# Moving the centring of V for the first two pairs from a TensorE matmul to VectorE and GpSimd

## The chip, the cores and the metric

The kernel runs on one core of one Trainium2 chip. The metric is the device time of one execution in microseconds (us). The engines are TensorE (PE in the profile), VectorE (DVE), ScalarE (ACT), GpSimd (POOL) and SyncE (SP), which here issues the DMAs.

## The reference

Eight sequences of 256 tokens with 512 features pass through one block. For each sequence: `x = x + mlstm(layernorm(x), ctx, ctx)` and then `x = x + ffn(layernorm(x))`.

- `mlstm` has 16 heads of 32 features. Gates come from `[q, k, v] @ Wi` and `@ Wf`; a cumulative sum of log-sigmoids and a running maximum give a decay matrix D; the scores `q k^T / sqrt(32)` are multiplied by D, divided by a normaliser, and multiplied with V. Each head's output of 32 features is then normalised (mean taken off, divided by the root of the variance) and multiplied by `ln_scale`.
- `ffn` has weights of 4 bits with a scale per group of 128: `silu(x Wg^T) * (x Wu^T)`, 1408 wide, then `Wd`, then division by the root mean square.

Because the mean over a head's 32 output features is taken off, the kernel takes the mean over each head's 32 features off V beforehand: the mean of the output is then zero.

## The kernel before, in words

The eight sequences are worked in four pairs (512 tokens, four tiles of 128 tokens). One call of `iteration(p, q, n)` on each engine has 22 half-steps `h`: in it the attention of pair `p` (eight units `u` of four heads each), the feed-forward of the pair before, `q`, and at its end the first part of the next pair, `n` (norm, transposes, gates, scans). The calls are (0, None, 1), (1, 0, 2), (2, 1, 3), (3, 2, None), (None, 3, None). Each engine has its own program in a fixed order written out by hand, and the engines meet at semaphores.

What the change touches:

- Pairs 2 and 3 centre V so: `v_means` on VectorE (L1275) sums each head's 32 features of `ctx_sb` and scales the sums by -1/32; `centre_v` on GpSimd (L514) adds them to `ctx_sb` and writes `v_sb`, in four instructions of 128x512.
- Pairs 0 and 1 centre V otherwise: a matrix `centre` is made by GpSimd at the start (`centring`, L490), TensorE multiplies the transposed context by it (`centre_v`, L907, 16 matmuls of 128x128 fp32), and ScalarE copies the four banks to `v_sb` (`read_v`, L664).
- `keep_busy(count)` on TensorE (L1168) is matmuls whose result is not used. They stand where TensorE would otherwise wait.
- `decode_up(i)` on VectorE (L1466, by `decode`, L1459) turns packed 4-bit weights to 16-bit values in three instructions. Four of eight come before `iteration(0, None, 1)`.
- `mask(p, u)` on GpSimd (L526) zeroes what lies above the diagonal of the decay matrix (L532, twice) and makes `vw` from `v_sb` (L543, twice). VectorE's `products` (L1322, L1329) wait for it, and so does TensorE's `state_sums` (L959).
- `scans(0)` on VectorE (L1296) make the running sums; its `nm_ready` (L1310) starts TensorE's `spread_first` (L1157) and SyncE's spreading of `negm`.
- `read_scales` (L776) and `fetch_exp` (L680) on ScalarE convert scales and fetch the table for Exp.

Of the kernel before, what the change touches and what calls it, by code (L numbers as in the profile page):

```python
# [32 lines left out]
P = 128  # L33
# [76 lines left out]
def xattn_ffn(nc, x, ctx, ctxT, w_gates, b_gates, ln_scale, gu_bytes, gu_scales, dn_bytes, dn_scales, out):  # L110
# [6 lines left out]
    with es:  # L117
# [28 lines left out]
        own_rows = sb("own_rows", [P, HG, DH + 1])  # L146
        centre = sb("centre", [P, P])
        later = sb("later", [P, 2, HG, DH + 1])
# [82 lines left out]

        def bank_v(p, tt):
            return pf[:, (0, 2)[tt]] if p == 0 and tt < 2 else pq[:, 1] if p == 0 and tt == 3 else \
                po[:] if tt == (3 if p else 2) else pf[:, tt]

        def bank_y(p, n):
# [38 lines left out]
        vmean_ready = sem("vmean_ready")  # L275
        centre_ready = sem("centre_ready")
        vc_done = sem("vc_done")
        v_ready = sem("v_ready")
# [191 lines left out]
        def _(pool):  # L470
# [18 lines left out]

            def centring():  # L490

                heads = centre[:].rearrange("q (h d) -> q h d", d=DH)
                pool.memset(centre[:], -1.0 / DH).then_inc(centre_ready, 1)
                pool.wait_ge(centre_ready, 1)
                pool.affine_select(out=heads, in_=heads, compare_op=ALU.is_ge, fill=0.0, base=0,
                                   pattern=[[-DH, HG], [0, DH]], channel_multiplier=1).then_inc(centre_ready, 1)
                pool.wait_ge(centre_ready, 2)
                pool.affine_select(out=heads, in_=heads, compare_op=ALU.is_ge, fill=0.0, base=DH - 1,
                                   pattern=[[DH, HG], [0, DH]], channel_multiplier=-1).then_inc(centre_ready, 1)
                pool.wait_ge(centre_ready, 3)  # L500
                pool.tensor_tensor(centre[:], centre[:], ident[:], ALU.add).then_inc(centre_ready, 1)

            def gate_weights():
# [9 lines left out]

            def centre_v(p):  # L514
                pool.wait_ge(am_ready, 2 * p + 2)
                take_wait(pool)
                pool.wait_ge(vmean_ready, p - 1)
                pool.wait_ge(s_ctx, 16 * p + 16)
                pool.wait_ge(pv_done, UNITS * p)
                for tt in range(TT):  # L520
                    m = vmean[:, 1, tt * NH:(tt + 1) * NH].unsqueeze(2).to_broadcast([P, NH, DH])
                    pool.tensor_tensor(v_sb[:, tt, :, 0:DH],
                                       ctx_sb[:, tt].rearrange("q (h d) -> q h d", d=DH), m, ALU.add
                                       ).then_inc(v_ready, 1)
# [68 lines left out]
            def iteration(p, q, n):  # L593
# [13 lines left out]
                if q is None:  # L607
                    by_ln_scale(p)
                    residual1(p)
                    norm2(p)  # L610
                    return
                gated(q, FT - 1)
# [19 lines left out]

            setup()
            centring()
            rstd1(0)
            gate_weights()
            mask(0, 0)
            iteration(0, None, 1)
            for p in range(1, PAIRS - 1):
# [6 lines left out]
        def _(act):  # L646
# [10 lines left out]
            def norm1(p):  # L657
# [4 lines left out]
                last.then_inc(xn_ready, 1)  # L662

            def read_v(p):  # L664

                if p == 1:
                    act.wait_ge(pv_done, UNITS)
                for tt in range(TT):
                    act.wait_ge(vc_done, TT * p + tt + 1)
                    act.activation(v_sb[:, tt, :, 0:DH], bank_v(p, tt).rearrange("q (h d) -> q h d", d=DH), ACT.Copy  # L670
                                   ).then_inc(v_ready, 1)

# [118 lines left out]
            def iteration(p, q, n):  # L791
# [37 lines left out]
                if n is not None:  # L829
                    read_xT(n)  # L830
                    if q is None:
                        read_v(n)
                if p is not None and q is not None:
# [17 lines left out]
            softplus(0)  # L851
            read_v(0)
            fetch_exp()
            read_scales()
            exps(0, 0, 0)
# [11 lines left out]
        def _(pe):  # L867
# [38 lines left out]

            def centre_v(p):  # L907

                pe.wait_ge(centre_ready, 4)
                if p == 1:  # L910
                    pe.wait_ge(o_read, UNITS)
                for tt in range(TT):
                    for k in range(KT):
                        last = pe.matmul(bank_v(p, tt)[:, k * P:(k + 1) * P], xT[:, KT + k, tt * P:(tt + 1) * P],
                                         centre[:], start=True, stop=True)
                    last.then_inc(vc_done, 1)

            def turn_back(p):
# [40 lines left out]
            def state_sums(p, q, u):  # L959

                hg, b = u // 2, u % 2
                pe.wait_ge(vw_ready, 2 * UNITS * p + 2 * u + 2)
                if u == 0 and p < 2:
                    pe.wait_ge(s_ctx, 16 * p + 16)
                if p == 0:
# [60 lines left out]
            def turn_y(p):  # L1026
                pe.wait_ge(yn_ready, p + 1)
                if p == 0:
                    pe.wait_ge(v_ready, 2 * TT)
                if p < PAIRS - 1:  # L1030
# [126 lines left out]
            def spread_first(half):  # L1157

                if half == 0:
                    pe.wait_ge(v_ready, TT)  # L1160
                    pe.wait_ge(nm_ready, 1)
                for hh in range(2):
                    r = 2 * half + hh
                    last = pe.matmul(pf[:, 2 * half + 1, hh * S:(hh + 1) * S],
                                     ident[0:ROWS, r:r + 1].to_broadcast([ROWS, P]), nm[:], start=True, stop=True)
                last.then_inc(bc_done, 1)
# [8 lines left out]
            def iteration(p, q, n):  # L1175
# [27 lines left out]
                if n is not None:  # L1203
                    if q is None:
                        keep_busy(21)
                    turn_x(n)
                    gate_sums(n)
                    if q is None:
                        centre_v(n)
                        keep_busy(16)  # L1210
                if q is not None:
# [13 lines left out]
            gate_sums(0)  # L1225
            centre_v(0)
            keep_busy(10)
            spread_first(0)
# [11 lines left out]
        def _(dve):  # L1240
# [34 lines left out]
            def v_means(p):  # L1275

                dve.wait_ge(s_ctx, 16 * p + 16)
                step(dve.tensor_reduce(vmean[:, 0], ctx_sb[:].rearrange("q t (h d) -> q (t h) d", d=DH),
                                      AX.X, ALU.add))
                dve.tensor_scalar(vmean[:, 1], vmean[:, 0], -1.0 / DH, None, ALU.mult).then_inc(vmean_ready, 1)  # L1280
# [213 lines left out]
            def iteration(p, q, n):  # L1494
# [29 lines left out]
                if q is None:  # L1524
# [7 lines left out]
                    low_yT(p)  # L1532
                    read_a(n)
                    return
                if q is not None:
# [35 lines left out]
            input_rows(0)  # L1571
            for i in range(UP_FIRST, UP_EARLY):
                decode_up(i)
            scans(0)
            read_a(0)
            norm1_sums(1)
            iteration(0, None, 1)
            dve.wait_ge(sc_ready, 2)

# [41 lines left out]
```

## Time and profile before

| | us |
|---|---|
| median of 3 runs | 519.88 (519.51 to 520.72) |
| the profiled execution | 519.88 |
| its span, first to last instruction | 518.2 |

| engine | busy us | share of the span |
|---|---|---|
| PE | 488.7 | 94% |
| DVE | 392.6 | 76% |
| POOL | 328.4 | 63% |
| ACT | 299.2 | 58% |

Busy time of a whole engine doesn't tell what a moved instruction costs; the timelines of the stretch around it do. In a timeline row the first number is the start, the second the time, then engine, line, operation, tile written <- tiles read, and shapes; `x4` means that four such instructions are merged; a bracket at the end tells how long the engine was idle before, and what ended that.

### The profile page before, as it was taken

The numbers are of one execution on the slowest core, as the hardware profiler recorded it, in microseconds if no ns is written. First come the engines' busy times: TensorE is split into PE (matmuls) and PEld (weight loads), VectorE is DVE, ScalarE is ACT, GpSimd is POOL, SyncE is SP. The second block draws the span as 40 slices with busy tenths as digits, with TensorE's granted clock in tenths as the row PEclk, the third lists the DMA queues.
The fourth block names the chain that finished last, engine by engine and source line by source line (L and its number), as shares of the span: only waits on it lengthen the run. The fifth ranks groups of instructions, "written<-read, shape, count | busy, mean of one in ns | idle before, by whom it ended". The sixth has DMA issues, their size and how long they took to land.

```text
span 518.2 us, 8362 instructions
## 1 busy us (share of the span) xinstructions
PE 488.7 (94%) x2821; PEld 290.4 (56%) x2821; DVE 392.6 (76%) x690; ACT 299.2 (58%) x648; POOL 328.4 (63%) x368
## 2 busy tenths in 40 slices
PE   8899989589999899999999999999999989999996
PEld 3668766347666344567775445477774444444442
DVE  5968999779888988378888899378888952999411
ACT  1558764588776252588877245588875123877210
POOL 3025565088886764578887883778877771999610
PEclk9979999899999999999999999999999999999999
DMA  8685064372103300267006000663000000200011
GB/s 273 197 253 193 1 217 171 112 279 64 38 1 116 128 2 1 84 244 245 2 3 243 1 0 4 216 239 116 2 0 3 20 20 20 102 0 2 1 41 40
DMA packets 18507, 47.81 MB, mean 92 GB/s; under 512 B 1696, under 2 KB 4640, under 8 KB 17440
## 3 DMA queue, kind: packets, MB, share of 16 engines
q1 hardware_dynamic: 18464, 47.28, 26.4%
q8 instruction: 22, 0.36, 0.3%
q14 instruction: 21, 0.17, 0.1%
HBM read 37.31 MB, written 4.33 MB: 80 GB/s over the span
## 4 chain that ended last, share of the span: by engine, by line
PE 66%; DVE 20%; ACT 5%; issue 4%; POOL 3%; DMA 1%; SPq 0%; DVEq 0%; POOLq 0%; ACTq 0%
PE pf L1152 19%; PE pf L1088 12%; PE pf L1126 7%; PE pq L955 5%; PE po L1017 3%; PE pq L1111 3%; PE pf L1111 3%; DVE ffn L1430 3%; ACT dmat L715 3%; DVE ffn L1434 2%; DVE dmat L1329 2%; PE pq L1022 1%; DVE th L1442 1%; PE pq L903 1%; DVE w_down L1491 1%
## 5 line engine op out<-in xcount | busy, mean ns | idle before, releaser
L573 POOL TENSOR_TENSOR ffn<-ffn,ts 128x512 f32<-128x512 f32 x88 | 119.6, 1365 | 40.1 <-DVE ffn L1434 37.2
L1088 PE MATMUL pf<-yT,gu_val 128*128 128x512 f16 x464 | 135.9, 381 | 2.9 <-ACT ts L749 1.1
L1152 PE MATMUL pf<-w_down,hT 128*128 128x512 f32 x264 | 115.9, 595 | 1.7 <-DVE w_down L1491 1.7
L749 ACT ACTIVATE ts<-pf,gu_scale 128x512 f32<-128x512 f32 x134 | 85.1, 684 | 9.6 <-PE pf L1088 4.8
L1152 PEld LDWEIGHTS pf<-w_down,hT 128*128 128x128 f32 x264 | 49.3, 190 | 62.6 <-issue 57.5
L715 ACT ACTIVATE dmat<-negm,aT 128x128 f32<-128x128 f32 x248 | 77.6, 392 | 1.9 <-DMA negm<-negm_dram 1.9
L1088 PEld LDWEIGHTS pf<-yT,gu_val 128*128 128x128 f16 x464 | 56.0, 127 | 35.1 <-DVE ffn L1434 3.9
L532 POOL TENSOR_SCALAR_AFFINE_SELECT dmat<-dmat 128x512 f32<-128x512 f32 x64 | 43.4, 692 | 43.8 <-ACT dmat L715 43.8
L578 POOL TENSOR_TENSOR hT<-ffn,th 128x512 f32<-128x512 f32 x44 | 57.8, 1317 | 15.2 <-DVE th L1442 15.2
L1017 PEld LDWEIGHTS po<-v_sb,dmat 128*128 128x128 f32 x384 | 63.1, 191 | 4.6
L1017 PE MATMUL po<-v_sb,dmat 128*128 128x33 f32 x384 | 58.3, 233 | 0.0
L1434 DVE SCALAR_TENSOR_TENSOR ffn<-pf,gu_scale,ffn 128x512 f32<-128x512 f32 x67 | 50.3, 751 | 7.2
L1430 DVE SCALAR_TENSOR_TENSOR ffn<-pf,gu_scale,ts 128x512 f32<-128x512 f32 x67 | 49.7, 742 | 3.5 <-ACT ts L749 3.1
L767 ACT ACTIVATE th<-pf 128x512 f32<-128x512 f32 x16 | 9.5, 592 | 68.2 <-PE pf L1152 40.6
L955 PE MATMUL pq<-xT 32*128 32x128 f32 x448 | 40.9, 301 | 1.8
L1442 DVE SCALAR_TENSOR_TENSOR th<-th,ffn 128x512 f32<-128x512 f32 x44 | 41.3, 944 | 0.1
L584 POOL TENSOR_SCALAR ms<-ssq 128x1 f32<-128x1 f32 x16 | 4.4, 275 | 57.2 <-ACT th L767 56.9
L1329 DVE SCALAR_TENSOR_TENSOR dmat<-pq,dmat 128x512 f32<-128x512 f32 x56 | 35.9, 682 | 4.4 <-PE pq L955 3.3
L1126 PE MATMUL pf<-w_down,hT 128*128 128x512 f32 x88 | 39.1, 592 | 0.0
L955 PEld LDWEIGHTS pq<-xT 32*128 32x128 f32 x448 | 30.1, 189 | 12.1 <-PE pq L955 7.0
L722 ACT ACTIVATE tok<-po 128x264 f32<-128x264 f32 x32 | 12.5, 391 | 35.2 <-PE pq L1022 25.4
L758 ACT ACTIVATE th<-ffn 128x512 f32<-128x512 f32 x44 | 27.5, 626 | 5.8 <-POOL ffn L573 5.8
(156 smaller groups left out, 795.4 us busy)
## 6 DMA issues: line engine op xcount, KB each, us to landing
negm<-negm_dram SPq DMA_DIRECT2D x31, 512.0 KB, 5.1
xT<-in_ctx_T SPq DMA_DIRECT2D x4, 1024.0 KB, 7.9
ctx_sb<-in_ctx SPq DMA_DIRECT2D x4, 1024.0 KB, 5.4
x_sb<-in_x SPq DMA_DIRECT2D x4, 1024.0 KB, 5.9
x_res<-x_sb SPq DMA_DIRECT2D x4, 1024.0 KB, 4.6
out<-x_res SPq DMA_DIRECT2D x16, 256.0 KB, 2.0
ffn<-in_x SPq DMA_DIRECT2D x3, 1024.0 KB, 9.2
ts<-in_gate_up_bytes SPq DMA_DIRECT2D x4, 352.0 KB, 9.4
```

The source lines that it names most:

```text
L573: pool.tensor_tensor(acc, acc, ts[:, h % TDEEP, 1], ALU.add).then_inc(tsum_ready, 1)
L578: pool.tensor_tensor(hT[:, j], acc_buf(q, 1, j), th[:, j % 2], ALU.mult).then_inc(h_ready, 1)
L715: last = act.activation(dmat[:, u % 2, half, c, hh], m[:, c * P:(c + 1) * P], ACT.Exp, bias=aT[:, c, bh:bh + 1])
L749: act.activation(ts[:, h % TDEEP, g], bank(q, h, g), ACT.Copy, scale=gu_scale[:, g * GU + o:g * GU + o + 1]).then_inc(t_ready, 1)
L955: last = pe.matmul(bank_qk(p, u, half)[:, c:c + P], xT[r, KT + hg, t0:t0 + P], xT[r, hg, t0:t0 + P], start=True, stop=True)
L1017: pe.matmul(po[:, col:col + DH + 1], dmat[:, u % 2, half, blk, hh], v_sb[:, 2 * b + blk, hg * HG + 2 * half + hh], start=True, stop=True)
L1088: ins = pe.matmul(bank(q, h, g), gu_val[:, h // 2 + h % 2 * FT, g], yT[:, part, g], start=(part == 0), stop=(part == 1))
L1126: last = pe.matmul(pf[:, tt], hT[:, j, tt * P:(tt + 1) * P], w_down[:, j], start=(j == 0), stop=(j == FT - 1))
L1152: last = pe.matmul(pf[:, tt], hT[:, j, tt * P:(tt + 1) * P], w_down[:, j], start=(j == 0), stop=(j == FT - 1))
L1430: dve.scalar_tensor_tensor(acc, bank(q, h, 2), gu_scale[:, 2 * GU + o:2 * GU + o + 1], ts[:, h % TDEEP, 0], ALU.mult, ALU.add).then_inc(ac ...
L1434: dve.scalar_tensor_tensor(acc, bank(q, h, 3), gu_scale[:, 3 * GU + o:3 * GU + o + 1], acc, ALU.mult, ALU.add).then_inc(acc_ready, 1)
L1442: dve.scalar_tensor_tensor(th[:, j % 2], th[:, j % 2], 1.0, acc_buf(q, 0, j), ALU.add, ALU.mult).then_inc(gg_ready, 1)
```

## The change

For pairs 0 and 1 it does what pairs 2 and 3 do already. `centre`, `centring`, TensorE's `centre_v` and ScalarE's `read_v` go. GpSimd's `centre_v(0)` stands in two halves around `mask(0, 0)`, and `centre_v(1)` at the end of `iteration(0, None, 1)`. `v_means(0)` stands between `input_rows(0)` and `scans(0)`, where `decode_up(3)` was; `decode_up(3)` moves behind `norm1_sums(1)`. `v_means(1)` stands behind `read_a(1)`. The counts of `keep_busy` go from 10 to 28 and from 16 to 36. ScalarE reads the scales before it fetches the table. TensorE's waits on the context's DMA and on `v_ready` before `spread_first` and `turn_y` go.

```diff
@@ -144,7 +144,6 @@
         vw = sb("vw", [P, 2, HG, DH + 1])
         state = sb("state", [P, 2, HG, DH + 1])
         own_rows = sb("own_rows", [P, HG, DH + 1])
-        centre = sb("centre", [P, P])
         later = sb("later", [P, 2, HG, DH + 1])
         decay = sb("decay", [P, 2, NH])
         yT = sb("yT", [P, 2, KT, TT * P], F16)
@@ -229,10 +228,6 @@
         def bank_state(p):
             return pf[:, 1] if p == 0 else pq[:, 1]
 
-        def bank_v(p, tt):
-            return pf[:, (0, 2)[tt]] if p == 0 and tt < 2 else pq[:, 1] if p == 0 and tt == 3 else \
-                po[:] if tt == (3 if p else 2) else pf[:, tt]
-
         def bank_y(p, n):
             return po[:] if n == 2 else pq[:, min(n, 2)]
 
@@ -273,8 +268,6 @@
         nb_ready = sem("nb_ready")
         xn_ready = sem("xn_ready")
         vmean_ready = sem("vmean_ready")
-        centre_ready = sem("centre_ready")
-        vc_done = sem("vc_done")
         v_ready = sem("v_ready")
         xT_done = sem("xT_done")
         xT_read = sem("xT_read")
@@ -487,19 +480,6 @@
                                    ).then_inc(const_ready, 1)
                 pool.wait_ge(const_ready, 7)
 
-            def centring():
-
-                heads = centre[:].rearrange("q (h d) -> q h d", d=DH)
-                pool.memset(centre[:], -1.0 / DH).then_inc(centre_ready, 1)
-                pool.wait_ge(centre_ready, 1)
-                pool.affine_select(out=heads, in_=heads, compare_op=ALU.is_ge, fill=0.0, base=0,
-                                   pattern=[[-DH, HG], [0, DH]], channel_multiplier=1).then_inc(centre_ready, 1)
-                pool.wait_ge(centre_ready, 2)
-                pool.affine_select(out=heads, in_=heads, compare_op=ALU.is_ge, fill=0.0, base=DH - 1,
-                                   pattern=[[DH, HG], [0, DH]], channel_multiplier=-1).then_inc(centre_ready, 1)
-                pool.wait_ge(centre_ready, 3)
-                pool.tensor_tensor(centre[:], centre[:], ident[:], ALU.add).then_inc(centre_ready, 1)
-
             def gate_weights():
 
                 pool.wait_ge(s_const, 16 * 2)
@@ -511,13 +491,14 @@
                 pool.wait_ge(var1_ready, p + 1)
                 pool.tensor_tensor(rs[:, 0], vv[:, 0], neghalf[:, 0:TT], ALU.pow).then_inc(rstd1_ready, 1)
 
-            def centre_v(p):
+            def centre_v(p, tiles=range(TT)):
                 pool.wait_ge(am_ready, 2 * p + 2)
                 take_wait(pool)
-                pool.wait_ge(vmean_ready, p - 1)
+                pool.wait_ge(vmean_ready, p + 1)
                 pool.wait_ge(s_ctx, 16 * p + 16)
-                pool.wait_ge(pv_done, UNITS * p)
-                for tt in range(TT):
+                if not (isinstance(p, int) and p == 0):
+                    pool.wait_ge(pv_done, UNITS * p)
+                for tt in tiles:
                     m = vmean[:, 1, tt * NH:(tt + 1) * NH].unsqueeze(2).to_broadcast([P, NH, DH])
                     pool.tensor_tensor(v_sb[:, tt, :, 0:DH],
                                        ctx_sb[:, tt].rearrange("q (h d) -> q h d", d=DH), m, ALU.add
@@ -608,6 +589,7 @@
                     by_ln_scale(p)
                     residual1(p)
                     norm2(p)
+                    centre_v(n)
                     return
                 gated(q, FT - 1)
                 if n is not None:
@@ -631,10 +613,11 @@
                 down_scale(q, 3)
 
             setup()
-            centring()
             rstd1(0)
             gate_weights()
+            centre_v(0, range(2))
             mask(0, 0)
+            centre_v(0, range(2, TT))
             iteration(0, None, 1)
             for p in range(1, PAIRS - 1):
                 iteration(p, p - 1, p + 1)
@@ -660,15 +643,6 @@
                     last = act.activation(xg[:, tt], xg[:, tt], ACT.Identity, bias=nb[:, tt:tt + 1],
                                           scale=rs[:, 0, tt:tt + 1])
                 last.then_inc(xn_ready, 1)
-
-            def read_v(p):
-
-                if p == 1:
-                    act.wait_ge(pv_done, UNITS)
-                for tt in range(TT):
-                    act.wait_ge(vc_done, TT * p + tt + 1)
-                    act.activation(v_sb[:, tt, :, 0:DH], bank_v(p, tt).rearrange("q (h d) -> q h d", d=DH), ACT.Copy
-                                   ).then_inc(v_ready, 1)
 
             def softplus(p):
 
@@ -828,8 +802,6 @@
                     down_squares(q, 1)
                 if n is not None:
                     read_xT(n)
-                    if q is None:
-                        read_v(n)
                 if p is not None and q is not None:
                     down_scaled(q, 1)
                 if n is not None:
@@ -849,9 +821,8 @@
 
             read_xT(0)
             softplus(0)
-            read_v(0)
+            read_scales()
             fetch_exp()
-            read_scales()
             exps(0, 0, 0)
             exps(0, 0, 1)
             floors(0)
@@ -903,17 +874,6 @@
                             last = pe.matmul(pm[r:r + DH, 0:S], w_gate[:, k, gate * DH:(gate + 1) * DH],
                                              xT[:, k, b * S:(b + 1) * S], start=(k == 0), stop=(k == 2 * KT - 1))
                 last.then_inc(g_done, 1)
-
-            def centre_v(p):
-
-                pe.wait_ge(centre_ready, 4)
-                if p == 1:
-                    pe.wait_ge(o_read, UNITS)
-                for tt in range(TT):
-                    for k in range(KT):
-                        last = pe.matmul(bank_v(p, tt)[:, k * P:(k + 1) * P], xT[:, KT + k, tt * P:(tt + 1) * P],
-                                         centre[:], start=True, stop=True)
-                    last.then_inc(vc_done, 1)
 
             def turn_back(p):
 
@@ -960,8 +920,6 @@
 
                 hg, b = u // 2, u % 2
                 pe.wait_ge(vw_ready, 2 * UNITS * p + 2 * u + 2)
-                if u == 0 and p < 2:
-                    pe.wait_ge(s_ctx, 16 * p + 16)
                 if p == 0:
                     if u > 0:
                         pe.wait_ge(state_ready, u)
@@ -1025,8 +983,6 @@
 
             def turn_y(p):
                 pe.wait_ge(yn_ready, p + 1)
-                if p == 0:
-                    pe.wait_ge(v_ready, 2 * TT)
                 if p < PAIRS - 1:
 
                     pe.wait_ge(xT_read, KT * (p + 2))
@@ -1157,7 +1113,6 @@
             def spread_first(half):
 
                 if half == 0:
-                    pe.wait_ge(v_ready, TT)
                     pe.wait_ge(nm_ready, 1)
                 for hh in range(2):
                     r = 2 * half + hh
@@ -1206,8 +1161,7 @@
                     turn_x(n)
                     gate_sums(n)
                     if q is None:
-                        centre_v(n)
-                        keep_busy(16)
+                        keep_busy(36)
                 if q is not None:
                     down(q, 2, range(FT))
                 if p is not None:
@@ -1223,8 +1177,7 @@
             keep_busy(34, po[:])
             turn_x(0)
             gate_sums(0)
-            centre_v(0)
-            keep_busy(10)
+            keep_busy(28, po[:])
             spread_first(0)
             turn_back(0)
             spread_first(1)
@@ -1275,8 +1228,8 @@
             def v_means(p):
 
                 dve.wait_ge(s_ctx, 16 * p + 16)
-                step(dve.tensor_reduce(vmean[:, 0], ctx_sb[:].rearrange("q t (h d) -> q (t h) d", d=DH),
-                                      AX.X, ALU.add))
+                g1.link(dve.tensor_reduce(vmean[:, 0], ctx_sb[:].rearrange("q t (h d) -> q (t h) d", d=DH),
+                                       AX.X, ALU.add))
                 dve.tensor_scalar(vmean[:, 1], vmean[:, 0], -1.0 / DH, None, ALU.mult).then_inc(vmean_ready, 1)
 
             def gate_rows(p):
@@ -1531,6 +1484,7 @@
                     scans(n)
                     low_yT(p)
                     read_a(n)
+                    v_means(n)
                     return
                 if q is not None:
                     gate(q, FT - 1)
@@ -1569,11 +1523,12 @@
                 decode_up(i)
             gate_rows(0)
             input_rows(0)
-            for i in range(UP_FIRST, UP_EARLY):
-                decode_up(i)
+            v_means(0)
             scans(0)
             read_a(0)
             norm1_sums(1)
+            for i in range(UP_FIRST, UP_EARLY):
+                decode_up(i)
             iteration(0, None, 1)
             dve.wait_ge(sc_ready, 2)
 
```

## Rows read from the trace of the kernel before

**Rows 1.** Chain of waits, start of the program: start us, us, what.
```profile
19.97 0.60 DVE yT L1462
...
22.20 0.43 DVE negm L1299
...
28.77 3.52 PE po L1172 x8
```
**Rows 2.** Timeline of VectorE around pair 2's v_means: start, us, instruction.
```profile
202.98 2.27 DVE L1278 TENSOR_REDUCE vmean<-ctx_sb 128x64 f32<-128x2048 f32 x1
...
205.40 0.41 DVE L1299 SCALAR_TENSOR_TENSOR negm<-negm 48x256 f32<-48x256 f32 x1
```
**Rows 3.** Tile ctx_sb, 0 to 30 us: its DMA, and us to landing.
```profile
L343 SPq DMA_DIRECT2D ctx_sb<-in_ctx x1: 442/442/442, 5.7 to 5.7; - x1
...
DMA to landing us min/median/max: 11.7/11.7/11.7
```
**Rows 4.** Timeline of GpSimd, 200 to 218 us.
```profile
212.28 4.06 POOL L522 TENSOR_TENSOR v_sb<-ctx_sb,vmean 128x512 f32<-128x512 f32 x4
```
**Rows 5.** Timeline of VectorE, 0 to 42 us.
```profile
30.56 0.17 DVE L1260 TENSOR_SCALAR vv<-mv 128x4 f32<-128x4 f32 x1 [0.27 <-DVE mv L1246]
33.99 1.29 DVE L1329 SCALAR_TENSOR_TENSOR dmat<-pq,dmat 128x512 f32<-128x512 f32 x2 [3.26 <-PE pq L955]
```
**Rows 6.** Timeline of VectorE, 44 to 70 us: one decode beside GpSimd.
```profile
59.67 0.96 DVE L1462 TENSOR_SCALAR yT<-x_res,shifts 128x704 int32<-128x704 int32 x1
...
61.68 0.89 DVE L1464 SCALAR_TENSOR_TENSOR ts<-yT 128x704 int32<-128x704 int32 x1
```
**Rows 7.** Line L1463 by itself: ns min/median/max, first and last start.
```profile
L1463 DVE TENSOR_SCALAR yT<-yT x12: 527/683/980, 12.7 to 70.3; 128x704 int32<-128x704 int32 x12
```
**Rows 8.** Timeline of GpSimd, 0 to 42 us.
```profile
28.06 0.64 POOL L532 TENSOR_SCALAR_AFFINE_SELECT dmat<-dmat 128x512 f32<-128x512 f32 x1 [15.82 <-ACT dmat L715]
...
29.69 0.55 POOL L543 TENSOR_TENSOR vw<-v_sb,dmat 128x66 f32<-128x66 f32 x2
32.46 0.63 POOL L532 TENSOR_SCALAR_AFFINE_SELECT dmat<-dmat 128x512 f32<-128x512 f32 x1 [2.22 <-ACT dmat L715]
```
**Rows 9.** Timeline of ScalarE, 0 to 42 us.
```profile
21.18 0.42 ACT L678 ACTIVATE negm<-negm 48x256 f32<-48x256 f32 x1
...
26.75 2.18 ACT L715 ACTIVATE dmat<-pf,aT 128x128 f32<-128x128 f32 x8 [1.45 <-DVE aT L1319]
```
**Rows 10.** Timeline of TensorE, 0 to 42 us.
```profile
21.40 2.32 PE L1172 MATMUL pf<-ident 128*128 128x512 f16 x10
24.96 1.10 PE L1164 MATMUL pf<-nm,ident 48*128 48x256 f32 x4 [1.24 <-DVE nm L1310]
```
**Rows 11.** Stretches of 2 us: PE, PEld, DVE, ACT, POOL busy, clock, DMA.
```profile
26.00:28.00 2.00, 2.00 (x14) 1.29 (x14) 1.46 (x4) 1.25 (x5) 0.00 (x0) 0.71 0.11 21
```
**Rows 12.** Timeline of TensorE, 66 to 112 us.
```profile
93.23 1.09 PE L1043 MATMUL pq<-ident,tok 128*128 128x128 f32 x8 [2.14 <-DVE tok L1404]
...
99.09 2.72 PE L1088 MATMUL pq<-yT,gu_val 128*128 128x512 f16 x6 [2.10 <-issue]
```
**Rows 13.** Timeline of VectorE, 66 to 112 us.
```profile
98.80 0.25 DVE L1319 COPY aT<-pf 128x96 f32<-128x96 f32 x1
101.95 0.75 DVE L1430 SCALAR_TENSOR_TENSOR ffn<-pq,gu_scale,ts 128x512 f32<-128x512 f32 x1 [2.91 <-PE pq L1088]
...
111.30 1.28 DVE L1329 SCALAR_TENSOR_TENSOR dmat<-pq,dmat 128x512 f32<-128x512 f32 x2
```
**Rows 14.** Timeline of GpSimd, 66 to 112 us.
```profile
103.72 1.59 POOL L573 TENSOR_TENSOR ffn<-ffn,ts 128x512 f32<-128x512 f32 x1 [13.66 <-DVE ffn L1434]
...
107.54 0.55 POOL L543 TENSOR_TENSOR vw<-v_sb,dmat 128x66 f32<-128x66 f32 x2
```
**Rows 15.** Line L562 by itself, as in rows 7.
```profile
L562 POOL TENSOR_TENSOR x_sb<-x_sb,tok x16: 1166/1192/1637, 81.5 to 419.8; 128x512 f32<-128x512 f32 x16
```
**Rows 16.** Line L543 by itself, as in rows 7.
```profile
L543 POOL TENSOR_TENSOR vw<-v_sb,dmat x64: 290/297/965, 29.7 to 381.0; 128x66 f32<-128x66 f32 x64
```

## The prediction, made before the changed kernel ran

> **What bounds the kernel now.** I read the page's busy shares first: TensorE has 94% of the span, but the edits lie only in the first 35 us and around 84 to 107 us, so the question is which engine ends last there. The chain of waits answers that. From 10 us to the first score matmuls it runs over VectorE: decodes, gate rows, scans; then over TensorE, the `keep_busy` before the first state sums included [rows 1]. From 73 to 96 us it is VectorE again without a break, then `low_yT` and the feed-forward's first matmuls. Then the timelines of each engine at these two places tell who is idle, and for how long. The reader is to see in them that GpSimd is idle for 15.82 us before its first mask [rows 8] and 13.66 us before its first sum [rows 14], that ScalarE waits 1.45 us before the first exponentials [rows 9], and that VectorE has one idle stretch in each place, 3.26 us before 33.99 [rows 5] and 2.91 us before 101.95 [rows 13].
>
> The profiled execution took 519.88, which is also the median of the three runs; 1.68 of it lies around the span of 518.2. I add what changes to 519.88.
>
> **Start of the program, VectorE.** Where `decode_up(3)` stood, from 19.97 to 22.20 [rows 1], 2.23 us, there is now `v_means(0)`. Pair 2's took 2.27 us for the reduction, and from its start to the start of the next instruction, which stands behind the scaling too, 205.40 - 202.98 = 2.42 us [rows 2]. So the scans start at 19.97 + 2.42 = 22.39 instead of 22.20: +0.19. They need ScalarE's logarithm as well, which ends at 21.60 [rows 9]; it isn't late. The context landed at about 17.4, 11.7 us after its issue at 5.7 [rows 3], so the reduction doesn't wait.
>
> `decode_up(3)` now stands behind `norm1_sums(1)`, which ended at 30.73 [rows 5], now at 30.92. It must be done before the first products, at 33.99 before, about 34.18 now. The gap is 3.26 us; the decode without company is 2.23, which ends at 33.15. But it has company: the second half of GpSimd's `centre_v(0)` begins at about 30.4. Of one decode beside GpSimd the trace shows 61.68 + 0.89 - 59.67 = 2.90 us [rows 6], so it ends at about 33.9 with its semaphore. The worst single instruction seen is 0.98 against 0.53 [rows 7]; were all three stretched by 0.45 it would be 3.6 us and the end 34.5. So the decode costs nothing from one side and 0.3 from the other; I take 0, as 2.90 is the nearest row. Without the 3.26 us of cover it would cost its 2.2 to 2.9 whole.
>
> A rule speaks against the change here. The row shows L1463 at 527 ns alone and up to 980 with GpSimd at work [rows 7]. The Trainium skill, "GPSIMD Engine Reference", section 8 (Key points), says that GpSimd shares its SBUF interfaces with VectorE, and that they contend where VectorE's instruction runs in a 2-port mode or has two SBUF inputs. By the rule decode and `centre_v` slow each other, but the reduction of `v_means` doesn't suffer; by the 527 ns alone the decode would end 0.7 us sooner. The trace agrees with the rule, and the sum is the same by both, since the decode is off the path unless it passes 34.18.
>
> **Start of the program, the others.** GpSimd: making `centre` goes, in idle time, 0. The first half of `centre_v(0)` waits for the second of `am_ready` (ScalarE needs `aT` from the same source at 26.75), so it starts at about 25.8 and takes half of 4.06 [rows 4], to 27.9; the first mask starts at 28.06 [rows 8], 28.25 now. Hidden by 0.3; if these adds were as slow as the slowest two-input add, 1.637 [rows 15], it would end at 29.1 and the second mask half, at 29.09, would hide most. The second half runs from 30.24 + 0.2 to 32.5, and the next mask starts at 32.46 [rows 8], 32.65 now. VectorE comes to that unit's products only behind the first unit's, 1.29 from 33.99 [rows 5], and a decode, so at 37.5; a microsecond there costs nothing. ScalarE: four copies go, and next it waits 1.45 us for `aT` [rows 9]; no gain. TensorE: the matmuls of `centre_v` and 10 `keep_busy` ended at 23.72 [rows 10]; 28 at 0.215 to 0.232 end between 23.8 and 24.3, before 25.15, when `nm` is ready. So the gain from the matmuls taken off TensorE is 0: what is late next is `nm`.
>
> TensorE's granted clock fell in the stretch 26 to 28 us, which has 0.71 on average [rows 11]; the following 8 `keep_busy` took 3.52 us [rows 1], where 10 took 2.32 just before [rows 10]: 0.44 us each and 0.23 each, so the fall is from 2.4 to 1.2 GHz. Before the fall it had idled 1.24 us [rows 10] and done narrow matmuls of 48 rows. The idle time is now about the same (24.0 to 25.15), so I expect the same fall. If the clock's return stays where it was, work that starts 0.19 late regains a part of it. I take +0.2 for the start as a whole, with 0.1 and 0.5 as ends (the 0.3 of the decode on top of 0.19).
>
> From the products at 33.99 on, each unit's exponentials wait for the unit before, so nothing downstream takes up the 0.2, down to the norm at 90 us.
>
> **Around 84 to 107 us.** TensorE: its 16 matmuls go, 36 `keep_busy` from 83.8 at 0.215 to 0.232 end between 91.5 and 92.2. `turn_y` starts at 93.23, having waited 2.14 for VectorE [rows 12]. 0. ScalarE's copies: 0, `softplus` waits for VectorE too. VectorE: `v_means(1)` starts at 98.80 + 0.25 = 99.05 [rows 13], and 2.42 plus a tail of about 0.1 end at 101.55; the first feed-forward sum starts at 101.95 after 2.91 us of waiting for TensorE. Hidden by 0.4; were it not, VectorE and what follows would be late by the rest.
>
> GpSimd: `centre_v(1)` starts with `vmean` at 101.6, takes 4.06 [rows 4], and ends at 105.7. The first sum started at 103.72 [rows 14]: it is 2.0 late. Behind the waiting instruction are queued `sum_t(0, 0)`, 1.59, `mask(1, 0)`, two halves of 0.64 [rows 8] and `vw`, 0.55: done at about 109.1 instead of 108.09 [rows 14]. The exponentials were what the mask waited for, which is why 2.0 becomes 1.0. VectorE asks for `vw` at 111.30 [rows 13], so 2.2 us of cover are left. Cost 0; without the cover, the delay whole. The lower bound isn't below nothing for any of these, since no path ends with work that is taken away, but for the clock, below.
>
> Sum: 519.88 + 0.19 and 0.0 = 520.1.
>
> **Rivals.**
>
> Late masks of pair 1 (slower). GpSimd's `centre_v(1)` is stretched by VectorE. With 1.637 an instruction [rows 15] it takes 6.55 and ends at 108.15; then 1.59 + 1.28 + twice 0.965, the slowest half of a `vw` [rows 16], end at about 112.9, which is 1.6 after 111.30, and VectorE, which is nearly full from there to 168 us, doesn't get it back: 519.9 + 0.2 + 1.6 = 521.7. It decides from 2.2 us of extra time on. For it: GpSimd's 128x512 adds took 1.59 in this very stretch [rows 14]. Against it: pair 2's took 1.02 each.
>
> The clock falls elsewhere (slower). If it stays up past 26.8 and falls at 34 instead, the first values, 3.9 us of mostly TensorE work from 33.99, run at half clock for about 3 us and lose 1.5: 521.5. For it: TensorE would wait for `vw` at 30.4 once its `keep_busy` is short.
>
> The clock stays up (faster). Then 8 `keep_busy` end 1.7 us sooner, and the products can start when VectorE is free, at 33.2 to 33.9 instead of 34.18: -0.3 to -1.0. At 99.09 six matmuls took 2.72 [rows 12], again at half clock; there too up to 1.3 could come. The first alone gives 519.5, both 518.2. For it: some more `keep_busy` before each. Against it: the idle stretch itself (2.10 us before 99.09) is untouched.
>
> **Chances.** Mine 0.68 (519.7 to 520.5); clock up at the first place only, 0.10, at both 0.07; late masks 0.09; clock elsewhere 0.06. About 0.2%, 1.04 us, is what a measurement can tell from no change. The first case and the clock up once lie within it (0.78, of which I give 0.03 to each side for causes I haven't seen); faster 0.07 + 0.03 = 0.10; slower 0.15 + 0.03 = 0.18. The range reaches down to the clock kept up once and up to short of the late masks: 519.1 to 521.3.
>
> **What would show it.** In the changed profile: the scans' first instruction at about 22.4; `decode_up(3)` between 30.9 and 34.0 and the products at 34.0 to 34.3; the first mask at 28.2; the clock low from about 27 to 33.5 and again near 98.5 to 102; `v_means(1)` ended before 101.7 and no new wait of VectorE on GpSimd between 105 and 125. I am wrong if products wait for `vw` in pair 1, or if the first values start before 33.5.

## The result and the profile after: 526.53 us, 1.2% slower

| | before | after |
|---|---|---|
| median | 519.69 us (518.21 to 520.72, 4 runs) | 526.53 us (525.7 to 543.2, 4 runs) |
| ratio | | 1.0121, 95% interval 1.0087 to 1.0156 |
| profiled execution, span | 519.88, 518.2 | 526.74, 525.0 |
| mean granted clock of TensorE | 0.990 | 0.979 |

The forecast was 520.1, no change; the kernel became 6.8 us slower by the medians and by the spans, 6.3 by the ratio. Some executions lie far above the others of the same kernel (543.2 here, 532.9 once among those of the kernel before); ratios leave such executions out, medians and the ranges in brackets hold them.

The chain of waits of the changed kernel, at the start (start us, us, what), is to be read against [rows 1]:

```profile
20.62 2.30 DVE vmean L1231
...
23.14 0.33 DVE negm L1252
...
31.11 0.94 DVE vv L1213
32.05 1.38 DVE yT L1415
...
33.45 0.85 DVE yT L1416
...
34.32 0.90 DVE hT L1417
...
35.46 0.70 DVE dmat L1282
```

`v_means(0)` stands where the decode stood, and is about 0.2 longer. But from 27.2 to 35.2 the chain now runs over VectorE, where before it ran over TensorE: `norm1_sums(1)`, and from 32.0 on `decode_up(3)`. The products (L1282) come at 35.46 instead of 33.99. What TensorE did meanwhile stands in its timeline:

```profile
32.80 1.12 PE L915 MATMUL pf<-xT 32*128 32x128 f32 x10
36.30 0.61 PE L946 MATMUL po<-v_sb,dmat 128*128 128x33 f32 x2 [2.37 <-DVE dmat L1282]
...
41.89 0.65 PE L930 MATMUL pf<-vw,ctx_sb 128*128 128x132 f32 x2
...
49.68 0.39 PE L930 MATMUL pf<-vw,ctx_sb 128*128 128x132 f32 x2
```

It stood idle for 2.37 us before the first values (L946), and the first two of these now take 0.61 together instead of 0.38. The same instructions of the kernel before had no listed wait:

```profile
34.83 0.38 PE L988 MATMUL po<-v_sb,dmat 128*128 128x33 f32 x2
```

The reader is to see the reason in the stretches of 4 us (us busy of PE, PEld, DVE, ACT and POOL, then granted clock, DMA share, GB/s), first after, then before:

```profile
30.00:34.00 4.00, 3.79 (x32) 2.06 (x30) 3.79 (x6) 2.27 (x8) 3.76 (x6) 0.79 0.98 324
34.00:38.00 4.00, 1.70 (x8) 1.54 (x9) 3.68 (x7) 1.45 (x2) 1.88 (x3) 0.64 0.98 244
38.00:42.00 4.00, 4.00 (x20) 3.63 (x19) 2.19 (x4) 0.00 (x0) 0.00 (x0) 0.50 1.07 420
42.00:46.00 4.00, 3.93 (x24) 3.08 (x24) 3.04 (x6) 3.87 (x10) 1.62 (x2) 0.50 0.31 109
46.00:50.00 4.00, 4.00 (x23) 3.47 (x23) 1.29 (x2) 0.23 (x2) 0.80 (x3) 0.65 0.36 123
50.00:54.00 4.00, 3.93 (x39) 3.46 (x38) 3.02 (x6) 3.87 (x10) 2.19 (x3) 1.00 0.09 18
```

```profile
30.00:34.00 4.00, 3.85 (x25) 2.20 (x23) 0.36 (x3) 2.99 (x9) 1.25 (x3) 0.54 1.04 345
34.00:38.00 4.00, 3.88 (x34) 3.47 (x34) 3.90 (x7) 0.80 (x2) 0.78 (x3) 1.00 1.00 267
38.00:42.00 4.00, 3.93 (x40) 3.42 (x38) 3.83 (x8) 3.91 (x10) 2.13 (x3) 1.00 1.04 412
42.00:46.00 4.00, 3.83 (x35) 3.12 (x35) 3.36 (x8) 3.40 (x10) 1.76 (x4) 1.00 0.42 161
```

In finer stretches the clock of the changed kernel is at half (1.2 GHz) from 28.3 to 31.7 and from 35.1 to 48.7, and again from 106.7 to 110.3; that of the kernel before from 26.8 to 33.7 and from 98.5 to 101.9. The second of the three is new: 13.6 us in which the first two units' values run at half speed, although TensorE is listed as busy for nearly all of it from 36.3 on. ScalarE's reads of the units (L696, L722 before) show what that costs:

```profile
31.73 2.44 ACT L689 ACTIVATE dmat<-negm,aT 128x128 f32<-128x128 f32 x8 [1.83 <-DMA negm<-negm_dram]
...
42.13 0.39 ACT L696 ACTIVATE tok<-po 128x264 f32<-128x264 f32 x1 [6.68 <-PE pq L953]
...
49.88 0.39 ACT L696 ACTIVATE tok<-po 128x264 f32<-128x264 f32 x1 [3.77 <-PE pq L953]
...
54.55 0.39 ACT L696 ACTIVATE tok<-po 128x264 f32<-128x264 f32 x1 [0.69 <-PE pq L953]
```

The same reads before:

```profile
37.92 0.39 ACT L722 ACTIVATE tok<-po 128x264 f32<-128x264 f32 x1 [3.20 <-PE pq L995]
...
42.60 0.39 ACT L722 ACTIVATE tok<-po 128x264 f32<-128x264 f32 x1 [0.69 <-PE pq L995]
```

Laid against each other (each row counts from the end point of the row above it), every microsecond of the difference finds a place:

| from, to | before | after | difference |
|---|---|---|---|
| start to first running sum (L1301, L1254) | 22.65 | 23.50 | +0.85 |
| to the first products | 11.34 | 11.96 | +0.62 |
| to the first unit's read | 3.93 | 6.67 | +2.74 |
| to the second unit's read | 4.68 | 7.75 | +3.07 |
| to pair 1's `read_a` | 56.20 | 55.53 | -0.67 |
| from there to the end | 419.40 | 419.59 | +0.19 |
| sum | 518.20 | 525.00 | +6.80 |

Of the first 0.85, 0.65 had come before `v_means`: VectorE waited for the fourth tile of `x` (0.66 us for its DMA; before, it had no such wait). So 5.8 of the 6.8 lie in the two units in which the clock was low.

Pair 1's part did what it should. VectorE and GpSimd there, to be read against [rows 13, 14]:

```profile
105.57 2.28 DVE L1231 TENSOR_REDUCE vmean<-ctx_sb 128x64 f32<-128x2048 f32 x1
107.88 0.20 DVE L1233 TENSOR_SCALAR vmean<-vmean 128x64 f32<-128x64 f32 x1
108.01 0.75 DVE L1383 SCALAR_TENSOR_TENSOR ffn<-pq,gu_scale,ts 128x512 f32<-128x512 f32 x1
...
117.45 1.29 DVE L1282 SCALAR_TENSOR_TENSOR dmat<-pq,dmat 128x512 f32<-128x512 f32 x2
118.66 1.62 DVE L1395 SCALAR_TENSOR_TENSOR th<-th,ffn 128x512 f32<-128x512 f32 x1
```

```profile
108.16 4.51 POOL L503 TENSOR_TENSOR v_sb<-ctx_sb,vmean 128x512 f32<-128x512 f32 x4 [11.37 <-DVE vmean L1233]
112.63 1.26 POOL L554 TENSOR_TENSOR ffn<-ffn,ts 128x512 f32<-128x512 f32 x1
...
115.03 1.00 POOL L524 TENSOR_TENSOR vw<-v_sb,dmat 128x66 f32<-128x66 f32 x2
```

`vw` is done at 116.03, 1.4 us before VectorE asks for it at 117.45.

### The profile page after: what moved, and what is told of

Same layout as the page of the kernel before. It is cut to its first block, busy times and chain, and to the rows that moved or that the text cites. A ratio compares the mean times of both kernels' runs of the same rounds, so it can differ in the third digit from the quotient of the medians.

```text
span 525.0 us, 8313 instructions
## 1 busy us (share of the span) xinstructions
PE 493.0 (94%) x2795; PEld 290.8 (55%) x2795; DVE 400.2 (76%) x694; ACT 294.6 (56%) x640; POOL 335.0 (64%) x372
## 4 chain that ended last, share of the span: by engine, by line
PE 66%; DVE 21%; issue 4%; ACT 4%; POOL 3%; DMA 1%; SPq 0%; DVEq 0%; POOLq 0%; ACTq 0%
PE pf L1108 19%; PE pf L1044 12%; PE pf L1082 7%; PE pq L915 5%; PE po L975 3%; PE pq L1067 3%; PE pf L1067 3%; DVE ffn L1383 3%; ACT dmat L689 2%; DVE ffn L1387 2%; DVE dmat L1282 2%; PE po L946 2%; PE pf L1127 2%; DVE th L1395 2%; PE pq L980 1%
## 5 line engine op out<-in xcount | busy, mean ns | idle before, releaser
L513 POOL TENSOR_SCALAR_AFFINE_SELECT dmat<-dmat 128x512 f32<-128x512 f32 x64 | 45.4, 725 | 30.8 <-ACT dmat L689 30.6
L1395 DVE SCALAR_TENSOR_TENSOR th<-th,ffn 128x512 f32<-128x512 f32 x44 | 42.8, 979 | 0.1
L1282 DVE SCALAR_TENSOR_TENSOR dmat<-pq,dmat 128x512 f32<-128x512 f32 x56 | 35.9, 682 | 2.2 <-POOL vw L524 1.8
L696 ACT ACTIVATE tok<-po 128x264 f32<-128x264 f32 x32 | 12.5, 390 | 42.1 <-PE pq L980 26.1
L1127 PE MATMUL pf<-ident 128*128 128x512 f16 x105 | 32.9, 405 | 0.0
```

The costliest lines, as they stand in the source:

```text
L1395: dve.scalar_tensor_tensor(th[:, j % 2], th[:, j % 2], 1.0, acc_buf(q, 0, j), ALU.add, ALU.mult).then_inc(gg_ready, 1)
```

## The experiments

My theory after the result: the loss is TensorE's clock. VectorE's late product leaves TensorE idle just before the first values, the clock falls, and the values' short matmuls (33 columns, with few `keep_busy` between) don't bring it back for some 7 to 14 us. Rival: the moved work costs by itself, `v_means` and GpSimd's adds on the path at the start, and the clock is a side effect. Second rival: pair 1's part costs. All ratios are against the kernel before, run beside; its medians in the comparisons of e1 to e14 were 518.5 to 519.1 (519.69 in that of the changed kernel). Where a median and a ratio say different things, the ratio counts. The last column is what the one profile of each kernel showed between 20 and 90 us.

| kernel | median us | ratio, 95% interval | low clock at |
|---|---|---|---|
| changed kernel | 526.53 | 1.0121 (1.0087 to 1.0156) | 28.3-31.7, 35.1-48.7 |
| e1 pair 0 only | 524.48 | 1.0083 (1.0048 to 1.0117) | 32.8-39.8 |
| e2 pair 1 only | 519.33 | 1.0011 (0.9989 to 1.0033) | nowhere |
| e3 changed, filled | 521.57 | 1.0051 (1.0028 to 1.0074) | 27.0-30.6 |
| e12 changed, filled twice | 520.20 | 1.0029 (1.0008 to 1.0051) | 27.4-31.0 |
| e4 decode back before the scans | 523.50 | 1.0080 (1.0056 to 1.0105) | 26.6-37.0 |
| e5 `v_means(0)` late | 527.56 | 1.0172 (1.0138 to 1.0206) | 26.8-30.4, 33.6-47.4 |
| e14 e5, filled | 526.82 | 1.0151 (1.0118 to 1.0183) | 32.4-39.4 |
| e7 before, decode moved | 520.76 | 1.0021 (0.9988 to 1.0054) | 32.8-46.6 |
| e13 e7, filled | 517.95 | 0.9987 (0.9971 to 1.0003) | nowhere |
| e8 before, VectorE late | 536.53 | 1.0318 (1.0237 to 1.0399) | 28.2-31.8, 35.0-59.2 |
| e9 e8, filled | 522.62 | 1.0068 (1.0043 to 1.0093) | 67.2-70.8 |
| e10 before without 8 `keep_busy` | 523.82 | 1.0066 (1.0042 to 1.0090) | 28.0-45.4, 58.8-89.6 |
| e11 before, filled | 521.81 | 1.0053 (1.0024 to 1.0082) | 27.2-34.2 |

### Which pair

e1 has pair 0 of the changed kernel and pair 1 of the one before; e2 the other way round. In e1, with `centring`, TensorE's `centre_v` and `read_v` back for pair 1:

```diff
                     norm2(p)
-                    centre_v(n)
                     return
...
                     read_a(n)
-                    v_means(n)
                     return
...
-                        keep_busy(36)
+                        centre_v(n)
+                        keep_busy(16)
```

> Pair 0 is centred as in the changed kernel, pair 1 by TensorE as in the kernel before (16 keep_busy there). My theory: all of the loss is at the start, where the first products came at 35.46 us instead of 33.99, TensorE then stood idle for 2.4 us and its clock was at 1.2 GHz from 35.2 to 48.8 us. It expects 525.5 to 527. The rival that pair 1's part costs (GpSimd's four adds before its first sums) expects 519.5 to 521 here.

> Pair 1 is centred as in the changed kernel (36 keep_busy), pair 0 by TensorE as in the kernel before. The theory of the start expects no change, 519 to 520.5. The rival that pair 1's part costs expects 523 to 526.

e1 measured 524.48 (520.12 to 542.66, 10 runs), e2 519.33 with an interval that holds 1. The second rival falls. e1 came out lower than I expected and wide; its profile had the clock low for 7 us instead of 13.6, and the second unit's read came 4.67 us after the first, as before. Yet TensorE had stood idle for longer than in the changed kernel, 3.61 us before the first values: the length of the wait alone doesn't set the price.

### The clock or the work

e3 puts matmuls without a use where TensorE stood idle, and changes nothing else:

```diff
                                 scores(p, q, VALUES[s] + 1, 1)
+                            if VALUES[s] == 0:
+                                keep_busy(12)
                             values_busy(VALUES[s])
```

> The changed kernel with 12 more keep_busy on TensorE between the scores of unit 1 and the first values, where it stood idle for 2.4 us. Nothing else is touched. The clock theory expects the clock to stay at 2.4 GHz from 35 us on and 5 us back: 520.5 to 522. The rival that the moved work itself (v_means, GpSimd's adds, the decode in front of the products) costs, the clock being a side effect, expects 526 to 528.

521.57 is 3.0 above the kernel before beside it, where the changed kernel was 6.8 above: more than half came back, by adding work. It is at the upper end of what the clock theory gave. TensorE's timeline and clock in it:

```profile
31.60 1.12 PE L915 MATMUL pf<-xT 32*128 32x128 f32 x10
32.65 2.76 PE L1127 MATMUL pf<-ident 128*128 128x512 f16 x12
35.55 0.38 PE L946 MATMUL po<-v_sb,dmat 128*128 128x33 f32 x2
```

```profile
34.00:38.00 4.00, 3.87 (x28) 2.77 (x26) 3.68 (x7) 0.19 (x1) 0.88 (x2) 1.00 1.02 297
38.00:42.00 4.00, 3.93 (x38) 3.38 (x38) 3.79 (x9) 3.35 (x10) 1.39 (x2) 1.00 0.96 383
```

The products came 12.43 us after the first running sum, not earlier than in the changed kernel (11.96); yet the first unit's read came 16.36 after it instead of 18.63. What stays against the kernel before (15.27) is 1.1 us: the late products themselves, since the values start 0.83 after the products, as before (0.84). From pair 1's `read_a` to the end it took 420.13 instead of 419.40, with the clock low from 98.8 to 105.7.

e4 takes the decode from in front of the products and puts it between `v_means(0)` and `scans(0)`:

```diff
             v_means(0)
+            for i in range(UP_FIRST, UP_EARLY):
+                decode_up(i)
             scans(0)
             read_a(0)
             norm1_sums(1)
-            for i in range(UP_FIRST, UP_EARLY):
-                decode_up(i)
```

> The changed kernel with decode_up(3) between v_means(0) and the scans instead of in front of the first products. The scans start 2.2 us later, and with them everything, but the products no longer wait for VectorE. Clock theory: no idle stretch before the first values, 5 to 6 us back and 2.2 lost: 521.5 to 524. The rival that v_means and the adds on GpSimd cost by themselves expects 2.2 more than the changed kernel: 528 to 529.

523.50, inside what the clock theory gave, and 5 under the rival's. The scans are 2.2 us later by construction, and the clock rose at 37.0, before the values.

### The wait without the change

e7 moves the decode in the kernel before, and nothing else; e8 instead leaves it and repeats it twice in front of the products, so that VectorE is late as in the changed kernel, without any other part of the change; e9 is e8 with the 12 `keep_busy` of e3.

```diff
 # e7
-            for i in range(UP_FIRST, UP_EARLY):
-                decode_up(i)
             scans(0)
             read_a(0)
             norm1_sums(1)
+            for i in range(UP_FIRST, UP_EARLY):
+                decode_up(i)
 # e8
             norm1_sums(1)
+            for _ in range(2):
+                decode(gu_words[:, QROW:2 * QROW], gu_bits[:, QROW:2 * QROW, 1], 1)
```

> The kernel before with decode_up(3) moved behind norm1_sums(1), and nothing else of the change. The scans start 0.5 us earlier (they then wait for the logarithm, which ends at 21.6); the decode has no company of GpSimd's adds there, takes 2.2 us and ends at 32.5, before the scores are done. My theory expects 517.5 to 519.5, no loss. The rival that the decode's new place alone is harmful expects 522 or more.

> The kernel before with the fourth decode done twice more behind norm1_sums(1) (its output is the same). VectorE comes to the first products at about 35.3 instead of 34.0, as in the changed kernel, without any other part of the change. The clock theory expects 1.3 us directly and several more by the clock: 521 to 526. If a late product costs only itself, 519.5 to 520.5.

> The kernel before with the fourth decode done twice more (532 to 544 us without the fill) and 12 keep_busy on TensorE between the scores of unit 1 and the first values. VectorE is exactly as late as there. If the late products act only through the idle TensorE and its clock, the fill gives nearly all back: 520 to 523. If the late VectorE costs by itself, it stays above 528.

e8 measured 536.53, beyond even my range: products 1.4 us later than in the kernel before, by their distance from the first running sum (12.77 against 11.34), cost 3.2%, or 16.5 us. TensorE had waited 3.13 us for them. Its clock stayed low for 24 us:

```profile
34.00:38.00 4.00, 0.90 (x5) 0.84 (x6) 3.90 (x7) 1.39 (x2) 2.12 (x4) 0.65 1.01 258
38.00:42.00 4.00, 4.00 (x20) 3.53 (x18) 2.95 (x5) 0.00 (x0) 0.00 (x0) 0.50 1.05 413
...
46.00:50.00 4.00, 4.00 (x18) 3.47 (x18) 1.88 (x3) 0.91 (x1) 1.60 (x3) 0.50 0.34 131
...
54.00:58.00 4.00, 4.00 (x20) 3.31 (x19) 2.48 (x4) 1.56 (x2) 1.78 (x3) 0.50 0.39 131
```

e9 has the same late VectorE (13.13 from the first running sum to the products) and measured 522.62:

```profile
34.00:38.00 4.00, 2.38 (x16) 1.30 (x14) 3.90 (x7) 1.75 (x3) 2.18 (x4) 1.00 0.99 240
38.00:42.00 4.00, 3.93 (x39) 3.39 (x38) 3.79 (x9) 1.73 (x6) 0.01 (x1) 1.00 1.05 400
```

This is the cleanest pair of the study: 12 matmuls nobody reads are worth 13 us by the ratios (1.0318 and 1.0068). TensorE was still idle for 1.62 us before the first values in e9; what it had done just before differs.

e7's median missed my 517.5 to 519.5: 520.76, from 517.03 to 530.76; its ratio, 0.9988 to 1.0054, doesn't tell it from the kernel before. In its profile the products came at 32.63, sooner than before and nearer to the first running sum (10.08 instead of 11.34), and the clock still fell at 32.8, within a wait of TensorE of 1.26 us that ended at 33.47. So in that execution the products weren't later than before, and the fall came all the same, with TensorE idle. That idle TensorE costs time with no engine late, e10 shows:

```diff
                             scores(p, q, SCORES[s], 0)
-                            keep_busy(8, po[:])
                             state_sums(p, q, SCORES[s])
```

> The kernel before without the 8 keep_busy in front of the first state sums; nothing is later on any other engine, and TensorE has 1.8 to 3.5 us less to do. If idle TensorE drops the clock in the first units, 523 or more in many runs. If a wait of TensorE costs only what waits for it, 517.5 to 519.

523.82 (520.83 to 538.39): no engine has more to do, TensorE less, and the time is 3.4 us longer by the ratio (1.0042 to 1.0090). In its profile TensorE waited 2.37 us before the first state sums. That profile has a span of 532.2, far above the median, so its row in the table shows how far the low clock can go, not what it did at the median.

### Fills, and the version with v_means late

> The kernel before with 12 keep_busy between the scores of unit 1 and the first values. In its profile the products were ready at 35.2, and 12 at 0.215 us end at about 36.5: 1.5 us are lost directly. Its clock did not fall at this place, so nothing comes back: 519.5 to 520.5. If the clock fell there in some of its runs too, the spread shrinks and the median stays at 518.5 to 519.5.

e11 is the fill of e3 in the kernel before: 521.81, worse than I expected (520.5 at most). In its profile the clock was back at 34.2 and TensorE not idle when the fill came, so the 12 stand in the way of the values, which start at 38.17, 3.25 after the products (0.84 before); the first unit's read is 17.63 after the first running sum instead of 15.27:

```profile
35.58 2.76 PE L1172 MATMUL pf<-ident 128*128 128x512 f16 x12
```

A fill where TensorE isn't idle is paid in full: 2.7 us by the ratio.

> The changed kernel with the 12 keep_busy as in e3_fill (521.57) and 6 more behind turn_back(1), where TensorE idles 2.1 us before pair 0's feed-forward and its clock fell at 98.5 to 107 us in the profiles. If that fall costs about 1 us, 520 to 521; if it costs nothing there, as VectorE's v_means(1) ends last anyway, 521.5.

e12, e3 with `keep_busy(6, pf[:, 2])` behind `turn_back(n)` at the end of `iteration(0, None, 1)`, measured 520.20; the clock didn't fall near 100 us in its profile. The ratio went from 1.0051 in e3 to 1.0029, with intervals that overlap, and the profile took 418.87 from `read_a` to the end where e3's took 420.13: it looks as if that fall cost about 1 us, but isn't shown.

e5 puts `v_means(0)` behind `read_a(0)` and the decode back to its old place; e14 is e5 with 8 `keep_busy` before the first values:

```diff
-            v_means(0)
+            for i in range(UP_FIRST, UP_EARLY):
+                decode_up(i)
             scans(0)
             read_a(0)
+            v_means(0)
             norm1_sums(1)
-            for i in range(UP_FIRST, UP_EARLY):
-                decode_up(i)
```

> The changed kernel with v_means(0) behind read_a(0) and decode_up(3) back in its old place, in front of the scans. The scans start at 22.2 us as in the kernel before; GpSimd's first two adds wait for v_means until about 29.1, vw is there at about 33.0 instead of 30.2, the products at about 34. Clock theory: no long idle stretch of TensorE before the first values: 518.5 to 521. The rival that v_means and the adds cost by themselves expects 525 to 527.

> e5_means_late (527.56), the changed kernel with v_means(0) behind read_a(0) and the decode in its old place, and 8 keep_busy in front of the first values. There the products came at 33.5, so not late at all, and it still lost 9 us. If the clock took them, 519 to 521.5. If v_means and GpSimd's adds at the start cost by themselves, it stays above 524.

Both came out against me: 527.56 where I expected 518.5 to 521, and 526.82 where I expected 519 to 521.5. e5 has its products at 33.51, 11.53 after the first running sum, on time, and lost at least as much as the changed kernel; e14 gained nothing that is clear of noise. Its TensorE timeline says why:

```profile
28.02 1.90 PE L1127 MATMUL po<-ident 128*128 128x512 f16 x8
33.11 0.81 PE L930 MATMUL pf<-vw,ctx_sb 128*128 128x132 f32 x2 [3.20 <-POOL vw L524]
...
36.40 3.33 PE L1127 MATMUL pf<-ident 128*128 128x512 f16 x8
...
42.07 0.47 PE L953 MATMUL pq<-state,xT 128*128 128x132 f32 x2
```

The wait had moved: TensorE idled for 3.20 us before the first state sums, for GpSimd's `vw` (1.55 in e5's profile), and the clock fell at 32.4, ahead of the fill, whose 8 matmuls then took 3.33 us. The fill stood behind the idle stretch instead of in it. Here the rival is partly right: `v_means` behind `read_a` makes `vw` late by itself (32.5 + 0.55 in e14, 30.2 before).

> The kernel before with decode_up(3) behind norm1_sums(1), as in e7_before_moved (520.76, 517.0 to 530.8, clock low from 32.8 to 46.6 us in its profile, although its products came at 32.6, earlier than before), and 7 keep_busy on TensorE in front of the first values. If the clock alone spoiled that move, 517 to 518.5, at or under the kernel before; if not, 520 and more.

e13, e7 with 7 `keep_busy` in the wait of TensorE: 517.95 (517.07 to 519.67, 12 runs), against 518.91 beside it. Its median is the lowest of all, but the interval of the ratio, 0.9971 to 1.0003, just holds no change, and it overlaps that of e7. So it looks as if the decode's move alone, with the fill, gave up to 1 us; it isn't shown.

## Why the prediction was wrong

- **VectorE's scans later by 0.19.** Right: from the start of `v_means` to the next instruction it was 2.43, 20.62 to 23.05, where I had 2.42.
- **`decode_up(3)` hidden, cost 0, at worst 0.3.** Mis-sized. It ran from 31.97 to 35.21, 3.24 us, near the bound of 3.6 that I had laid aside for the row of 2.90. Even the tiny addition before it (L1213) took 0.94 instead of 0.17 beside GpSimd's second pair of adds. The products came 0.62 later by both. The rule of the Trainium skill, "GPSIMD Engine Reference", section 8 (Key points), on the shared interfaces agrees with this trace: the decode stretched (L1415 at 1.45, against 0.57 alone), the reduction, which had no GpSimd beside it, took 2.29, pair 2's 2.27; that it would not suffer beside GpSimd no run shows.
- **TensorE's clock.** This is the step that failed. I wrote that the idle stretch before `nm` was about the same, "so I expect the same fall". I looked at the gap in front of the known fall, and not at the one behind the scores, which the decode's 3.26 us of cover had hidden: before, TensorE entered the values at 34.83 without a listed wait; after, it waited 2.37 us. The fall that I expected came too, at 28.3, and the costly one on top of it at 35.1. The nearest of my rivals was "the clock falls elsewhere", with a chance of 0.06 and a price of 1.5 us, worked out as one stretch of half clock; but it had the fall in place of the first one, and after a wait for `vw`, not for the products. The price was 5.8: the clock didn't come back with the values, since it stayed low through two units (35.1 to 48.7), and in e8 through 24 us.
- **The cover of 3.26.** It was no fixed room. Only 0.62 of the new wait is the products' delay; the rest is TensorE, which was through with unit 1's scores 1.64 sooner, counted from the first running sum (10.42 against 12.06), as its first low stretch lasted 3.4 us instead of 6.9. VectorE's idle time before the products thus hung on the low clock of the one profile that I read. In e2, whose start is that of the kernel before and whose clock didn't fall there, it is 0.85, with the products 8.93 after the first running sum, too little for any decode:

```profile
30.27 1.29 DVE L1325 SCALAR_TENSOR_TENSOR dmat<-pq,dmat 128x512 f32<-128x512 f32 x2 [0.85 <-PE pq L954]
```

- **GpSimd at the start, ScalarE, TensorE's matmuls: 0.** Right. GpSimd's adds ended at 28.72 and its first mask began at 28.84, 5.34 behind the first running sum (5.41 before), and ScalarE waited 3.52 us instead of 1.45 for `aT`.
- **Pair 1: 0.** Right, with less cover than I gave: `centre_v(1)` took 4.51 instead of 4.06, 1.4 us were left of 2.2, and `v_means(1)`, which I had hidden by 0.4, ended last before the first sum. From `read_a` to the end +0.19; e2 gives 1.0011.
- **The clock stays up, as a gain.** It wasn't the changed kernel's case, but in e2's profile it happened at the first place, with a span of 515.8. The kernel before has executions with the same mean clock, 0.997, and spans of 515.4 to 515.9, so it needn't be pair 1's doing.

Not measured: the changed kernel without `decode_up(3)` at all, since what reads its output would read nothing. What stays open is why e1 lost only one 7 us stretch in its profile where the changed kernel lost 13.6, and how the 2.6 us that e3 keeps by its ratio divide. In its profile the last thing that the products waited for was GpSimd's `vw`, so the decode may not be alone in the 1.1 us; and against executions of the kernel before in which the clock stays up, as in e2's profile, its products are 3.5 us late, not 1.1.

## What to carry to other kernels

When an instruction moves into the idle time of one engine, look at what the other engines do in that time: here an instruction in VectorE's 3.26 us of cover made TensorE wait, and waits of TensorE of 1.3 to 3.6 us in front of the first units came with 7 to 24 us at half clock and with losses of up to 16.5 us. Idle time read from one profile may also hang on the clock of that execution: it was 3.26 us in one and 0.85 in another of the same start. A forecast should list every wait of TensorE that the change makes longer and price a low clock by how long the following work would leave it low, not by one stretch. Work without a use pays only inside the wait: in front of the fall it gave 13 us (e9), behind it nothing that can be told from noise (e14), without a wait it cost 2.7 (e11).

## What was unexpected of the hardware

The clock stayed at 1.2 GHz for 13.6 us (changed kernel) and 24 us (e8) while TensorE, from 38 us on, was listed busy for 3.9 to 4.0 us of each 4. The work there is matmuls of 33 columns and of 32 rows, with `keep_busy` matmuls of 512 columns between; being listed as busy doesn't mean that the clock comes back. The same work, begun at 2.4 GHz, held it (kernel before, 34 to 62 us at 1.00). Nor did every wait bring a fall: in e9 TensorE idled for 1.62 us before the first values, and the clock stayed up until 67.2.
